# Alternating whole steps of a recurrence with other VectorE work, moving column sums on TensorE, and loading the next stage's operands inside the last unit

## The reference

```
x = x + mixer(layernorm(x))                  # a recurrence over time, 32 heads x 32 states
x = x + cross_attention(layernorm(x), ctx)   # 77 context rows, 16 heads
x = x + experts(layernorm(x))                # a shared expert and 3 of 15 routed ones
```

```
z = S * (z - dt * A * s + dt * Bz * u)
s = s + dt * z + dt * Bx * u
y = Cz . z + Cx . s
```

## Time and profile before

| | |
|---|---|
| median of 3 runs | 2998.26 us (2997.25 to 3001.26) |
| the profiled execution: its time, its span | 2998.96 us, 2997.1 us |
| busy: PE / DVE / ACT / POOL | 2731.3 / 2035.7 / 1017.1 / 286.9 us |
| mixer, from its first residual addition to the fifteenth | 409.3 to 1855.2 us |
| last residual addition of the mixer | 1911.5 us |
| mean granted TensorE clock | 0.961 of full speed |

### The profile page before, as it was taken

The page is one execution under the profiler, slowest core; times in us unless marked ns, Lnnn a source line. Parts: engine busy times, 40 slices in busy tenths (PEclk is TensorE's granted clock), DMA queues, the critical chain, the costliest instruction groups (busy, mean ns, idle before and its releaser), DMA issues. The chain is left out here.

```text
span 2997.1 us, 89339 instructions
## 1 busy us (share of the span) xinstructions
PE 2731.3 (91%) x37280; PEld 2096.9 (70%) x37280; DVE 2035.7 (68%) x6918; ACT 1017.1 (34%) x2107; POOL 286.9 (10%) x227
## 2 busy tenths in 40 slices
PE   7955999999999999999999999588979999999998
PEld 3434777877877887888778787433335667888887
DVE  7648999999999999999999999455565001111111
ACT  4633333333333333334333433133323222333332
POOL 0000000000000000000000000000000751434434
PEclk9977999999999999999999999689989999999999
DMA  8874344254334424442533342200016234777776
GB/s 278 233 205 108 89 119 111 59 130 107 98 77 125 108 73 114 109 118 55 138 106 90 85 127 82 85 1 1 1 32 254 99 106 113 195 201 204 194 194 184
DMA packets 254886, 360.38 MB, mean 120 GB/s; under 512 B 73131, under 2 KB 177596, under 8 KB 243772
## 3 DMA queue, kind: packets, MB, share of 16 engines
q1 hardware_dynamic: 232060, 329.86, 38.8%
q0 software_dynamic: 22464, 25.31, 4.0%
HBM read 265.15 MB, written 93.55 MB: 120 GB/s over the span
## 5 line engine op out<-in xcount | busy, mean ns | idle before, releaser
L677 PE MATMUL ring<-valt,wbc 128*128 128x256 f32 x4096 | 939.5, 386 | 28.2 <-DMA valt<-valt_scratch 27.2
L677 PEld LDWEIGHTS ring<-valt,wbc 128*128 128x128 f32 x4096 | 772.2, 192 | 138.0 <-issue 28.7
L835 ACT COPY bc<-ring 128x512 f32<-128x512 f32 x256 | 150.3, 587 | 757.4 <-PE ring L677 757.4
L997 DVE TENSOR_TENSOR uu<-phi,coef 128x64 f32<-128x64 f32 x2048 | 358.5, 215 | 2.3 <-issue 0.2
L1003 DVE TENSOR_TENSOR phi<-phi,uu 128x64 f32<-128x64 f32 x2048 | 358.0, 214 | 0.0
L2156 DVE TENSOR_SCALAR f_yr<-fp_y,f_meta 128x256 f32<-128x256 f32 x124 | 54.3, 479 | 422.6 <-PE fp_y L1966 422.6
L1966 PE MATMUL fp_y<-f_w,f_hT 128*128 128x256 f32 x992 | 230.7, 386 | 7.9
L2040 ACT ACTIVATE f_hT<-fp_h,f_b 128x256 f32<-128x256 f32 x248 | 117.6, 474 | 327.3 <-PE fp_h L1957 327.3
L1957 PE MATMUL fp_h<-f_xrt,f_w 128*128 128x256 f32 x992 | 226.1, 381 | 0.9 <-ACT f_xrt L2029 0.9
L1798 POOL DMA_INDIRECT out_dram<-f_yr,f_meta x124 | 192.6, 1554 | 350.8 <-DVE f_yr L2156 267.2
L1785 POOL COPY f_xn<-f_gk 128x32 f32<-128x32 f32 x3 | 0.7, 245 | 2324.9 <-DVE f_rowid L2137 2321.7
(11 more groups left out here) (235 smaller groups left out, 3836.3 us busy)
## 6 DMA issues: line engine op xcount, KB each, us to landing
f_w<-in_W_dram SPq DMA_DIRECT2D x128, 512.0 KB, 4.5
coef<-par_scratch SPq DMA_DIRECT2D x128, 256.0 KB, 5.8
fb<-fac_scratch SPq DMA_DIRECT2D x256, 128.0 KB, 3.0
fc<-fac_scratch SPq DMA_DIRECT2D x256, 128.0 KB
xg_scratch<-f_fill SPq DMA_DIRECT2D x16, 1032.0 KB, 17.4
f_xr<-xg_scratch SPq DMA_DIRECT2D x64, 258.0 KB, 4.9
vtok_scratch<-p_vtok SPq DMA_DIRECT2D x32, 512.0 KB, 7.9
dub<-vtok_scratch SPq DMA_DIRECT2D x16, 1024.0 KB, 5.6
```

The source lines that it names most:

```text
L677: mm = pe.matmul(ring[:, p % 2, v * UT:(v + 1) * UT], wbc[:, k, g, first + v, :], valt[:, u % 2, k, :], start=(k == 0), stop=(k == 3))
L835: nc.scalar.copy(bc[:, gp, first:first + 2, i // 2, :], o).then_inc(bc_ready, 1)
L997: made[k] = mark(V.tensor_tensor(uu[:, k].rearrange("p i (g b) -> p i g b", b=B), phi[:, t, ::-1, k, :].rearrange("p i (g b) -> p i g b", ...
```

## The change

Four things are done.

1. *Whole steps.* `uu` is laid out with the row index first, and 10 of the 64 steps of each unit but the first are made by two operations on both halves at once (`weave`), one call for the product and one for the sum. Calls are put between other operations: two steps around `post(u, 1)`, six among the eight scans of `accumulate`, the three operations of `post(u, 2)` and `factors`, one behind `mask(u, 2)` and one behind `mask(u, 3)`.
2. *Order in `post`.* The decay of the state now comes first, the gate's product second, the sum into `hc` third, and the sum waits for the first of them by its number.
3. *Sums behind products.* In `mixed_states` the skip product and the carried state open the bank, all 64 state products follow, and `summed(un, gn, 1)` comes behind them. The waits for `hpad_ready` and `dub_in` move to the first product that needs them.
4. *Loading ahead.* The tile `wbc` (the mixer's big weight) now lives for the whole program. When the last projected tile of the last unit is made, SP loads into it the 16 operands of the cross attention and 4 chunks of rows (the even ones of 8, whose rows were stored long before): 20 transfers. The mixer's block no longer waits for its last stores; the next block's SP does, and then loads the odd chunks. In the cross attention the statistics and roots are split into tiles 0 to 3, 4 to 11 and 12 to 31; the first root comes ahead of the copies of keys; two of the clearings come later. The experts keep `xnt` in the other half of `wbc`.

```diff
@@ mixer, SP
+                if not more:
+                    sp.wait_ge(ring_full, 4 * GP * NU)
+                    for dst, src in ahead.sources(d, x1):
+                        sp.dma_start(dst, src).then_inc(ahead.loaded, 16)
...
             store_x(NU - 1)
-            sp.wait_ge(x_out, 16 * B * NU)
@@ mixer, TensorE, mixed_states
-                pe.wait_ge(hpad_ready, 2 * n + 2)
                 if gp == 0:
-                    pe.wait_ge(dub_in, 16 * (u + 1))
                     if u > 0:
                         pe.wait_ge(x1_ready, u)
                 else:
                     pe.wait_ge(post_ready, n)
+                pe.matmul(yp[:, 0:UT].rearrange("p (b t) -> p t b", b=B), skip[:, gp, :], turns(valt[:, u % 2, gp, :]),
+                          start=True, stop=False, skip_group_check=True)
+                pe.matmul(yp[:, UT:2 * UT], ident[:], hc[:, gp].rearrange("p v i b e -> p (v i b e)"),
+                          start=False, stop=False, skip_group_check=True)
+                pe.wait_ge(hpad_ready, 2 * n + 2)
...
-                    if b == 0 and more:
-                        summed(un, gn, 1)
-                pe.matmul(yp[:, 0:UT].rearrange("p (b t) -> p t b", b=B), skip[:, gp, :], turns(valt[:, u % 2, gp, :]),
-                          start=False, stop=False, skip_group_check=True)
-                pe.matmul(yp[:, UT:2 * UT], ident[:], hc[:, gp].rearrange("p v i b e -> p (v i b e)"),
-                          start=False, stop=False, skip_group_check=True)
+                if more:
+                    summed(un, gn, 1)
+                if gp == 0:
+                    pe.wait_ge(dub_in, 16 * (u + 1))
@@ mixer, VectorE
+            def weave():
+                t = woven["t"]
+                if woven["made"] is None:
+                    if woven["last"] is not None:
+                        need(woven["last"])
+                    woven["made"] = mark(V.tensor_tensor(
+                        uu[:].rearrange("p i k (g b) -> p k i g b", b=B),
+                        phi[:, t, ::-1].rearrange("p i k (g b) -> p k i g b", b=B),
+                        coef[:, :, :, t * B:(t + 1) * B].unsqueeze(1).broadcast_to([P, 2, 2, G, B]), ALU.mult))
+                else:
+                    need(woven["made"])
+                    woven["last"] = mark(V.tensor_tensor(phi[:, t + 1], phi[:, t], uu[:], ALU.add))
+                    woven.update(t=t + 1, made=None)
+
+            def weave_end(t):
+                if woven["made"] is not None:
+                    weave()
+                assert woven["t"] == t
+                need(woven["last"])
...
                 if more:
-                    evolve(u + 1, 0, 16)
+                    evolve(u + 1, 0, 14)
+                    weave_from(14)
                     factors(n0 + 4)
-                post(u, 1, n0 + 4)
-                if more:
+                    weave()
+                    post(u, 1, n0 + 4, weave)
+                    weave_end(16)
                     evolve(u + 1, 16, 28)
-                mask(u, 2)
-                if more:
-                    evolve(u + 1, 28, 44)
-                    accumulate(u + 1)
-                post(u, 2, n0 + 4)
-                if more:
+                    weave_from(28)
+                    mask(u, 2)
+                    weave()
+                    weave_end(29)
+                    evolve(u + 1, 29, 42)
+                    weave_from(42)
+                    accumulate(u + 1, weave)
+                    post(u, 2, n0 + 4, weave)
                     factors(n0 + 5)
-                    evolve(u + 1, 44, 60)
-                mask(u, 3)
-                if more:
-                    evolve(u + 1, 60, L)
+                    weave()
+                    weave_end(48)
+                    evolve(u + 1, 48, 61)
+                    weave_from(61)
+                    mask(u, 3)
+                    weave()
+                    weave_end(62)
+                    evolve(u + 1, 62, L)
                     inputs(u + 1, 0)
@@ cross_attention, SP
+            sp.wait_ge(x_out, 16 * B * NU)
+            for u in range(1, XNU, 2):
+                sp.dma_start(xres[:, XA * u:XA * u + XA, :], x1v[:, XA * u:XA * u + XA, :]).then_inc(x_next if u == 1 else x_in, 16)
+            sp.wait_ge(x_in, 48)
@@ cross_attention, VectorE
-            stats(0, XF * XA)
-            dve.wait_ge(w_loaded, 16 * NW)
-            roots(0, XF * XA, 1)
+            stats(0, XA)
+            V.memset(mx[:], 0.0)
+            V.memset(rec[:], 0.0)
+            roots(0, XA, 1)
             normed(0)
...
+            stats(XA, XF * XA)
+            roots(XA, XF * XA, 2)
             normed(1)
```

More of the change, by code:

```diff
@@ L403, with mixer @@
 TC = UT // 4
-def mixer(nc, d, st, wbc, x, x1):
+def mixer(nc, d, st, wbc, x, x1, x_out, ahead):
     with ExitStack() as ctx:
@@ L474, in mixer @@
         x_in = sem("x_in")
-        x_out = sem("x_out")
         fac_out = sem("fac_out")
@@ L1008, in evolve, with weave_from, accumulate @@
                 need(chain[0])
-            def accumulate(u):
+            woven = {"t": 0, "made": None, "last": None}
+            def weave_from(t):
+                woven.update(t=t, made=None, last=None)
+            def weave():
[16 more added lines that the diff above has]
+                need(woven["last"])
+            def accumulate(u, pause=None):
                 for h in range(2):
@@ L1015, in accumulate @@
                         ins = V.tensor_tensor_scan(v[:, :, b], resetm[:], v[:, :, b], 0.0, ALU.mult, ALU.add)
-                ins.then_inc(cum_ready, 1)
+                        if h == 1 and b == B - 1:
+                            ins.then_inc(cum_ready, 1)
+                        if pause is not None:
+                            pause()
             def factors(n):
@@ L1087, in mask, with post @@
                     .then_inc(km_ready, 1)
-            def post(u, gp, read):
+            def post(u, gp, read, pause=None):
                 n = GP * u + gp
@@ L1166, in attention @@
         ("valt", (NU, P, 4, UT), F32), ("par", (UQ, 5, P, UT), F32), ("fac", (NU * GP, H, UT), F32))}
-    with nc.sbuf_tensor("wbc", [P, 4, G, 4, P], F32) as wbc:
-        projections(nc, d, x, st, wbc)
-        mixer(nc, d, st, wbc, x, x1)
+    projections(nc, d, x, st, wbc)
+    mixer(nc, d, st, wbc, x, x1, x_out, ahead)
 SK, DC = 77, 192
@@ L1192, with cross_attention @@
 XIDX = {k: i for i, k in enumerate(XRING)}
-def cross_attention(nc, d, x1, xres, mv2):
+def cross_attention(nc, x1, mv2, x_out, ahead):
     with ExitStack() as ctx:
@@ L1243, in cross_attention @@
         sump = ps("sum", [P, 512])
-        w_loaded = sem("w_loaded")
-        NW = 16
+        w_loaded = ahead.loaded
+        NW = 20
         set_ready = sem("set_ready")
-        x_first = sem("x_first")
         x_next = sem("x_next")
@@ L1601, with experts @@
 NB = NTOK // 512
-def experts(nc, d, xres, mv, out):
+def experts(nc, d, xres, mv, out, xnt):
     with ExitStack() as ctx:
@@ L2168, in program @@
     x1 = nc.dram_tensor("x1_scratch", (NTOK, DM), F32).ap()
-    attention(nc, d, d["x"].rearrange("b t m -> (b t) m"), x1)
-    with nc.sbuf_tensor("xres", [P, NT, DM], F32) as xres, nc.sbuf_tensor("mv2", [P, NT, 2], F32) as mv2:
-        cross_attention(nc, d, x1, xres, mv2)
-        experts(nc, d, xres, mv2, out)
+    with nc.sbuf_tensor("wbc", [P, 4, G, 4, P], F32) as wbc, nc.semaphore("x1_out") as x_out, \
+            nc.semaphore("cross_loaded") as loaded:
+        ahead = CrossOperands(wbc, loaded)
+        attention(nc, d, d["x"].rearrange("b t m -> (b t) m"), x1, wbc, x_out, ahead)
+        with nc.sbuf_tensor("mv2", [P, NT, 2], F32) as mv2:
+            cross_attention(nc, x1, mv2, x_out, ahead)
+            experts(nc, d, ahead.xres, mv2, out, ahead.spare.rearrange("p (k t) -> p k t", k=2))
 def layouts(inputs):
```

123 lines of the change are left out of this document (75 added, 48 removed).

## The result

The changed kernel took 2988.36 us (median of 12 runs, 2977.63 to 2996.61) beside 3000.39 us for the kernel before (12 runs). The ratio is 0.9964, with a 95% interval of 0.9951 to 0.9976: some 11 us faster, where 40 were forecast.

| from, to | before us | after us | change | forecast |
|---|---|---|---|---|
| 14 units, first to fifteenth residual | 1445.9 | 1440.5 | -5.4 | -26 |
| last unit | 56.3 | 61.2 | +4.9 | 0 |
| last residual to the last maximum of the scores | 282.9 | 268.6 | -14.3 | -12 |
| last maximum to the end | 802.7 | 802.6 | 0 | 0 |

What follows compares the result with a forecast made beforehand. VectorE and TensorE cycles of nearly equal length, 102.4 and 103.3 us a unit, were taken to bound the mixer. From 2998.96 us, -28 (15 units) and -12 (passage) gave 2959, 2958 for the median; range 2940 to 2980 us.

Steps and rivals of the forecast that it cites:

- Sums behind products: TensorE in the mixer: the second column sums no longer wait 0.59 us for the square in four groups, -2.4 us a unit.
- The rival with the pauses: TensorE's small products in the mixer: all but 0.4 of 2.4 us returns as pauses, unit 102.9 us, total 2981 us; chance 0.15.
- VectorE: Mixer: whole steps -1.1 us, uncovered ones +0.2, new order in post -0.3; -1.2 us a unit, to 101.2 us.
- the rule on the drain: VectorE's alternation: the skill says the next operation waits until the pipe is empty, so by it alternation could hide nothing.
- The unit: Mixer: VectorE and TensorE cycles of 101.2 and 100.9 us still touch; 101.4 us taken, 1.9 us less.
- Slack of the factors: Group 3's factors in the mixer: 2.6 us between ScalarE's end and VectorE's arrival covers sums that come 1.9 us later.
- The slower rival: Group 3's factors in the mixer: sums come too late, VectorE's unit becomes 105.4 us, total 3018 us; chance 0.04.
- The last unit: End of the mixer: the 20 loads now standing there cost 0, with +3 us as the other end.
- The passage: Mixer to cross attention: scores start 15.5 us earlier, less 2.5 us for the second normed and 1 for late tiles: -12 us.

Runs made afterwards that it cites:

- the two broken runs: The changed kernel with half of the state products ahead of the fourth projected tile, with whole steps 2967.29 us, without them and with post's old order 2986.94 us.
- the broken run: The changed kernel with half of the 64 state products ahead of the fourth projected tile, skip product and carried state behind the other half: 2967.29 us.

## Why the prediction was wrong

*Sums behind products: the failed step.* "The wait goes in all four groups: -2.4 us a unit, 103.3 - 2.4 = 100.9 us as above." The wait went in all four groups, and the order is what I wrote. The step that failed is the subtraction: it takes for granted that the work behind a removed wait simply starts earlier. TensorE was at the end of its supply of instructions in this run already before: its 17 pauses there, too, end 1.2 to 1.6 us behind a landed block. The wait of 0.59 us was time in which instructions came in. The sum also missed a gain, the 0.47 us a group by which the run is shorter without its waits. So 1.07 us a group were freed, not 0.59, and 0.85 came back as pauses. Net, this order is worth -0.2 us in a run. In the whole kernel it is worth nothing, or 3 to 5 us the wrong way, which the intervals do not tell from nothing. The clock's 54.6 us at its lower level, instead of 34.1, stood in no term.

*The rival with the pauses* (chance 0.15, 2981 us) names the mechanism that happened. That the unit came out at 102.9 us as written there is in part luck: 4.3 us a unit were freed and 3.4 came back, where it has 2.4 and 2.0, and the 14 units were read at a place where VectorE was ahead. My argument against it, that only 32 pauses stood in 56 groups, read a pause as something that a group has or has not. How near to one the groups without a pause were, the rows did not show. The Trainium skill, "Runtime: NRT & Kernel Launch", section "Instruction fetch mechanics", says that the fetch is hidden because issuing is slower. The trace disagrees in this run: 97.8 us of pauses in 53 places. I had put it beside the rival as what spoke against the cause.

*VectorE*: right in each price. 0.20 us for a whole operation beside a scan, 0.65 us for an uncovered step, -1.3 us a unit. That it is worth 20 us where TensorE is fed is shown by the two broken runs; in the change most of it goes into the wait for factors. Among the scans, whole products start 0.61 us behind the start of a scan that counts 0.69 us, and the next scan 0.18 us behind them, though they count 0.27: independent operations overlap. With the rule on the drain, cited there, the trace disagrees here too. The same section of the Trainium skill says further on that a next operation that is not held starts earlier; with that sentence the trace agrees.

*The unit*: 102.9 instead of 101.4 us. With the run broken, 101.7 us. So the sum of both halves comes near for a TensorE that gets its instructions, though that kernel has another order.

*Slack of the factors*: 2.6 us, taken as enough for 1.9 us of lateness. It was, in most units: VectorE waits for ScalarE's `nr` in 5 of 56 places, 8.5 us. ScalarE's own wait for the sums, 141.5 us, is not on the path by itself. The slower rival did not come.

*The last unit*: taken as 0 with +3 us as the other end, measured +4.9 us in one profile. With the loads in place it was +1.0 us with the old sums, +0.2 without whole steps, +1.9 with the loads alone and +2.8 in the broken run. None of these is above the 3 us allowed for. What the change has beyond them goes with TensorE's lag at the fifteenth residual: it ends the fourth tile 7.6 us behind that residual, before 1.3 us behind it. How the pauses of this one unit share in it stays open.

*The passage*: -12 us forecast, -14.3 measured, and right in its parts. The first scores come 18.6 us earlier, forecast 15.5, and 4.3 us of that are lost again up to the last maximum, forecast 3.5. The first maximum comes 26.3 us after the residual instead of 42.9. In the forecast the block's start at 1915 and the clearing and statistics add up to 1918.5, not 1919.2; nothing further hangs on it.

## What to carry to other kernels

Before a wait is subtracted, look at what refills during it. On an engine that works through hundreds of small instructions, a pause without a releaser in the middle of a row of equal operations can be a lack of instructions; the landings of the instruction blocks and the count of records between pauses tell. The remedy here was to spread the small instructions between large ones, not to pack them. Price each saving on one engine against the other engine's state: the same whole steps were worth 5 to 10 us or 20. Ask what a piece of work covered where it stood before: the last states, moved into one wait, opened another. And a transfer that is moved pays at the place it moves to: moved ahead, 1 MB of coefficients cost 40 us in the change and 64 in the broken run.

## What was not expected of the hardware

- TensorE got through 260 records of products, and as many of weight loads, in 4.4 us (the mean of the 9 runs of the change without a pause above 0.3 us), and could not keep this up: 53 pauses of 0.8 to 4.7 us in 14 units. Each ended 1.2 to 1.7 us behind the landing of a 16 KB block of instructions, whose own record takes 0.9 to 1.5 us, and stood at the same place of a stretch of 256 records.
- The seven longest ones, 3.9 to 4.7 us, stand where data transfers fill the DMA engines (busy share 0.8 to 0.9 in the 6 us ahead, about 1.0 from the stop on). In all seven the record of the block begins only 1.4 to 2.1 us after the engine had stopped; in the one above from 1033.82 to 1035.49, just as the data transfers drained. That one delays the other is argued from this, and not shown.
- Busy time of TensorE is not work: with the same products it was 1341.95 us in the change and 1356.85 us in the faster broken run.
- A pause can cost clock as well: 13 stretches at the lower level in the 14 units of the change, each at a pause of 1.7 us or more.
